# The second stage's last norm moved into the state-space stage, and a new order of weight casts and of the first unit

## The reference, cut to what matters

```python
x = _layernorm(x + _L0_attn_ref(x, ...))   # A
x = _layernorm(x + _L0_ffn_ref(x, ...))    # B
x = _layernorm(x + _L1_attn_ref(x, ...))   # C
x = _layernorm(x + _L1_ffn_ref(x, ...))    # D

# C: proj = x @ in_proj_w.T, split into gate (8192), xBC (8192 + 2*8*128) and dt (128 heads)
# xBC: causal convolution with 4 taps along the sequence, then silu; split into x, B, C
# dt = clip(softplus(dt + dt_bias)); cs = cumsum(dt * A) within chunks of 128 tokens
# scores = (C . B of the same group) * exp(cs_l - cs_s); y = scores @ (x * dt) + state term + D * x
# out = (y * silu(gate), normalised per group of 1024 channels) @ out_proj_w.T
```

## Time and profile before

| | |
|---|---|
| median of 3 runs | 2188.53 us (2187.5 to 2189.29) |
| profiled execution | 2190.99 us |
| its span | 2188.9 us |
| PE busy | 2121.9 us (97%) |
| VectorE busy | 1721.2 us (79%) |
| ScalarE busy | 1239.7 us (57%) |
| GpSimd busy | 688.5 us (31%) |
| mean granted PE clock | 0.987 |

### The profile page before, as it was taken

The page is one execution under the profiler, slowest core; times in us unless marked ns, Lnnn a source line. Parts: engine busy times, 40 slices in busy tenths (PEclk is TensorE's granted clock), DMA queues, the critical chain, the costliest instruction groups (busy, mean ns, idle before and its releaser), DMA issues. The chain is left out here.

```text
span 2188.9 us, 35859 instructions
## 1 busy us (share of the span) xinstructions
PE 2121.9 (97%) x10933; PEld 1691.8 (77%) x10933; DVE 1721.2 (79%) x2943; ACT 1239.7 (57%) x2216; POOL 688.5 (31%) x419
## 2 busy tenths in 40 slices
PE   9999999989999999999999999999999999988997
PEld 7888778868777777777777777777777777766775
DVE  7554446468778888898888888888888888888886
ACT  3222225433377677677767767677777767753232
POOL 5644334311122323324233333324233333330000
PEclk9999999999999999999999999999999999999999
DMA  5312404123231212222132122222221221212433
GB/s 191 113 51 87 159 7 138 58 55 114 98 102 51 91 52 67 73 69 68 49 92 61 55 78 64 68 64 77 61 71 58 68 83 49 74 38 97 144 123 108
DMA packets 126578, 176.40 MB, mean 81 GB/s; under 512 B 17748, under 2 KB 83796, under 8 KB 126068
## 3 DMA queue, kind: packets, MB, share of 16 engines
q1 hardware_dynamic: 126452, 175.07, 25.6%
HBM read 165.72 MB, written 9.31 MB: 80 GB/s over the span
## 5 line engine op out<-in xcount | busy, mean ns | idle before, releaser
L72 PE MATMUL bank<-xT_hi,C_w_hi 128*128 128x512 f32 x1160 | 473.6, 408 | 7.9 <-POOL C_w_lo L1658 7.5
L73 PE MATMUL bank<-xT_lo,C_w_hi 128*128 128x512 f32 x1160 | 459.9, 396 | 0.0
L74 PE MATMUL bank<-xT_hi,C_w_lo 128*128 128x512 f32 x1160 | 459.8, 396 | 0.0
L1658 POOL TENSOR_TENSOR C_w_lo<-C_raw,C_w_hi 128x512 fp32r<-128x512 f32 x130 | 180.5, 1389 | 789.6 <-ACT C_w_hi L1752 746.2
L1365 DVE SCALAR_TENSOR_TENSOR C_acc<-bank,C_par,C_acc 128x510 f32<-128x510 f32 (+2 forms) x384 | 281.2, 744 | 60.4 <-ACT C_acc L1712 37.7
L1481 DVE TENSOR_TENSOR C_decay<-C_decay,C_cb 128x512 f32<-128x512 f32 x384 | 291.9, 789 | 4.8 <-ACT C_decay L1838 4.8
L72 PEld LDWEIGHTS bank<-xT_hi,C_w_hi 128*128 128x128 f32 x1160 | 220.4, 190 | 62.7 <-POOL C_w_lo L1658 8.8
L74 PEld LDWEIGHTS bank<-xT_hi,C_w_lo 128*128 128x128 f32 x1160 | 220.1, 190 | 51.7
L73 PEld LDWEIGHTS bank<-xT_lo,C_w_hi 128*128 128x128 f32 x1160 | 220.9, 190 | 45.3
L72 PE MATMUL bank<-C_out_hi,C_yg_hi 128*128 128x512 f32 x512 | 202.1, 395 | 7.4 <-DVE C_yg_lo L1451 4.0
L74 PE MATMUL bank<-C_out_hi,C_yg_lo 128*128 128x512 f32 x512 | 201.3, 393 | 0.0
(11 more groups left out here) (268 smaller groups left out, 4326.8 us busy)
## 6 DMA issues: line engine op xcount, KB each, us to landing
C_raw<-in_Cxg SPq DMA_DIRECT2D x65, 512.0 KB, 3.6
C_cs_second<-cs_rows SPq DMA_DIRECT2D x64, 512.0 KB, 4.7
C_raw_out<-in_Cout SPq DMA_DIRECT2D x64, 256.0 KB, 2.8
ahead_raw<-in_D SPq DMA_DIRECT2D x32, 512.0 KB, 3.6
front_raw<-in_A SPq DMA_DIRECT2D x20, 512.0 KB, 4.3
B_stat_raw<-in_D SPq DMA_DIRECT2D x16, 512.0 KB, 3.6
ahead_raw<-in_D SPq DMA_DIRECT2D x32, 256.0 KB, 2.6
cb_rows<-C_decay SPq DMA_DIRECT2D x8, 768.0 KB, 3.2
```

Source lines behind the costliest of these rows:

```text
L72: pe.matmul(out, lh, rh, start=start, stop=False)
L73: pe.matmul(out, lh, rl, start=False, stop=False)
L74: return pe.matmul(out, ll, rh, start=False, stop=stop)
L1658: e.tensor_tensor(w_lo[:, slot, :], raw_at, f32(w_hi[:, slot, :]), ALU.subtract).then_inc(lo_done, 1)
```

## The change

Three things. (1) Stage B ends after its last sums, with 8 filler matmuls in place of 12; the norm of its second half is done in stage C with a new `HalfNorm`, `early`. PE makes dt and tile 0 for the first half of the tokens, then the transposes of the norm, waits for all low parts, and makes dt and tile 0 for the second half. (2) VectorE casts the weights of tile i + 2 right behind the convolution of tile i, ahead of the other steps of that place, and tile 2's ahead of the first convolution. The first unit's x weights are cast ahead of tile 15's taps. (3) In unit 0 the correlation products of group 7 are moved between the two halves of the convolution; ScalarE does its second silu after the decays, the second group of exponentials (`second_exp`) after the gate silus, and waits for the store of group 7 only ahead of the exponentials that overwrite its buffer; PE makes the masked products between the two halves of the gate product.

```diff
@@ -737,7 +737,7 @@
             half_sum(1)
-            if kind == "A":
+            if kind != "D":
                 return
 ...
@@ -745,9 +745,6 @@
                 norms[1].scale(v, t)
-            if kind != "D":
-                for k in range(KT):
-                    norms[1].low(v, k, sh.bank[k])
 ...
@@ -955,13 +952,11 @@
                 a2_copy(1)
+            if kind != "D":
                 return
 ...
                 norms[1].scale_shift(a, t)
-            if kind != "D":
-                for k in range(KT):
-                    norms[1].high(a, k, sh.bank[k])
 ...
@@ -1107,9 +1102,7 @@
             if kind == "B":
-                keep_busy(pe, sh, sh.bank[4], 12)
-                for k in range(KT):
-                    norms[1].turn(pe, k, sh.bank[k])
+                keep_busy(pe, sh, sh.bank[4], 8)
     if kind == "B":
 ...
@@ -1174,6 +1167,7 @@
         norm = HalfNorm(sh, ctx, "CN", 0)
+        early = HalfNorm(sh, ctx, "CE", 1)
         bank = sh.bank
 ...
@@ -1247,6 +1241,7 @@
         MS_BANK = 7
+        EARLY_BANK = (6, 7, 2, 3)
 ...
@@ -1523,9 +1518,17 @@
+            for t in range(HT):
+                early.stats_of(v, t, False)
+            early.spread(v)
             v.wait_ge(S.dtw_in, 16)
             v.tensor_copy(w_hi[:, 1, :], raw_out[:, 0, :]).then_inc(S.dtw_hi, 1)
+            early.invert(v)
+            for t in range(HT // 2):
+                early.scale(v, t)
             bc_high(0)
+            for k in range(KT):
+                early.low(v, k, bank[EARLY_BANK[k]])
             v.memset(ones[:, :], 1.0).then_inc(S.ones_set, 1)
 ...
@@ -1545,17 +1548,19 @@
             dt_next = dt_steps()
+            bc_high(1)
             for i in range(2 * GROUPS):
-                if i + 1 < 2 * GROUPS:
-                    bc_high(i + 1)
+                if i == 0:
+                    bc_high(2)
                 bc_conv(i)
+                if 0 < i < 2 * GROUPS - 2:
+                    bc_high(i + 2)
                 if i in (1, 2, 3):
 ...
                     move_cb(i // 2 - 1)
-            move_cb(GROUPS - 1)
             v.wait_ge(S.par_in, 16)
 ...
@@ -1564,6 +1569,8 @@
                 for h in range(2):
+                    if u.first and h == 1:
+                        move_cb(GROUPS - 1)
                     v.wait_ge(S.tap, U * 2 + (h + 1))
 ...
@@ -1725,6 +1732,11 @@
+            early.root(a)
+            for t in range(HT // 2, HT):
+                early.scale_shift(a, t)
+            for k in range(KT):
+                early.high(a, k, bank[EARLY_BANK[k]])
             a.wait_ge(S.consts_in, 32)
 ...
@@ -1761,14 +1773,14 @@
                     chunk_ends()
+                if i == 2 * GROUPS - 1:
+                    a.wait_ge(S.in_bc, 4 * GROUPS - 2)
+                    x_weights(0, 0)
                 bc_tap(i, 0)
 ...
                 bc_silu(i, 0)
-                if i == 2 * GROUPS - 1:
-                    a.wait_ge(S.in_bc, 4 * GROUPS - 2)
-                    x_weights(0, 0)
             bc_silu(2 * GROUPS - 1, 1)
 ...
@@ -1820,14 +1832,14 @@
-
                 for h in range(2):
                     for b in range(BATCH):
+                        if u.first and h == 1 and b == 2:
+                            a.wait_ge(S.cb_stored1, 8 * GROUPS)
                         if h == b == 0:
 ...
                                 a.wait_ge(S.cb_stored0, 8 * GROUPS)
-                                a.wait_ge(S.cb_stored1, 8 * GROUPS)
                             a.wait_ge(cs_in[u.j], (u.U - u.j) * 8 + 16)
 ...
@@ -1837,6 +1849,9 @@
                                  bank[6 + h][:, :].rearrange("p (b l) -> p b l", b=BATCH), ACT.Exp).then_inc(S.decays, 1)
+
+            def second_exp(u):
+
                 for h in range(2):
 ...
@@ -1864,15 +1879,21 @@
                 x_silu(u, 0)
-                x_silu(u, 1)
                 if not u.first:
+                    x_silu(u, 1)
                     y_high(u, 0)
 ...
                 decay_exp(u)
+                if u.first:
+                    x_silu(u, 1)
+                else:
+                    second_exp(u)
                 gate_silu(u, 0)
 ...
                 gate_weights(u.U + 1, 1 - u.j)
+                if u.first:
+                    second_exp(u)
                 if not u.first:
 ...
@@ -1897,10 +1918,10 @@
         def _(pe):
-            def in_bc(i):
+            def in_bc(i, halves=(0, 1)):
                 s = i % 2
                 pe.wait_ge(S.bc_w_lo, i + 1)
-                for h in range(2):
+                for h in halves:
                     wait(pe, S.bc_conv, 6 * (i - 2) + 3 * h + 3)
 ...
@@ -1937,8 +1958,14 @@
                 products(pe, bank[4 + h][:, :], 1, h).then_inc(S.dt_mm, 1)
+                in_bc(0, (h,))
+                if h == 0:
+                    for k in range(KT):
+                        early.turn(pe, k, bank[EARLY_BANK[k]])
+                    pe.wait_ge(early.x_ready, KT)
             for i in range(2 * GROUPS):
-                in_bc(i)
+                if i:
+                    in_bc(i)
                 if i in (5, 7, 9, 11, 13):
 ...
@@ -2068,12 +2095,11 @@
                 in_g(u, 0)
-                if u.group_ended:
+                if u.first:
+                    seg(u, 0)
+                if u.group_ended or u.first:
                     seg(u, 1)
                 in_g(u, 1)
-                if u.first:
-                    seg(u, 0)
-                    seg(u, 1)
                 if not u.first_pair:
 ...
```

## The result

| | before | after |
|---|---|---|
| median of the runs | 2188.30 us (2186.13 to 2190.19, 9 runs) | 2182.66 us (2179.84 to 2185.45, 9 runs) |
| profiled execution, span | 2190.99, 2188.9 | 2183.42, 2181.3 |
| mean granted clock | 0.987 | 0.990 |

The ratio is 0.9974, with 95% between 0.9966 and 0.9982: 5.6 us faster. The forecast was 2178.0, 10.5 us faster. The time lies inside the range for 8 in 10 (2172 to 2183), near its upper end, and outside the forecast's own 2175.5 to 2180.5. In the profiled pair the difference is 7.6 us.

What follows compares the result with a forecast made beforehand. PE was taken as the bound, with gaps and low clock to win: 2.3 us at the start plus 8.2 by the first units, 10.5 off 2188.53, median 2178.0; own range 2175.5 to 2180.5, 8 in 10 2172 to 2183.

Steps and rivals of the forecast that it cites:

- Part 1: Between stages B and C: norm beside C's first loads; with the tile-loop casts 5.4 us at full clock, 2.3 after low-clock charges.
- R: Start of C: the time PE goes on with the second half of dt after the norm's low parts, put at 457.8.
- the gap inside: Start of C: PE's wait for the norm's low parts before the second half of dt, about 2.1 us.
- Part 2: Loop over B and C tiles: earlier casts, VectorE late next; with the moved norm 5.4 us at full clock, 2.3 after charges.
- the wait for GpSimd at tile 4: Loop over B and C tiles: a GpSimd wait at tile 4 or behind would show the prediction wrong; no size given.
- Part 3: Before the first unit: x weights cast ahead of tile 15's taps, 3.30 us of wait plus 2.51 of clock, 5.8 us earlier.
- Part 4: First unit's new order: unit 1's transposes at 614.35, not 623.68; 9.3 us, less 1.1 of low clock, 8.2.
- A switch costs its drain too: ScalarE's two added table switches in the first unit cost 1.4 us each, leaving 7.7 us gained, 2180.8; chance 0.04.
- Nothing is won at the start: Start of C: gaps before R all drop the clock, VectorE's chain begins as late; 8.2 us gained, 2180.3; chance 0.17.
- The clock holds: All new PE gaps: none drops the clock level; 5.4 + 9.3 = 14.7 us gained, median 2173.8; chance 0.17.
- A new wait in the first unit: Store and load of group 7 take twice their 7.4 us; 3.1 us gained, 2185.4; chance 0.06.
- The low level stays: From start of C to second correlation product: clock never rises between new gaps, kernel 19 us slower, 2207; chance 0.04.

Runs made afterwards that it cites:

- part 1 alone: The kernel before with only the second-half norm moved into stage C and 8 fillers, old cast places and first unit; 2190.72 us, ratio 1.0009.
- after again: The changed kernel run once more with no edit; 2182.03 us, ratio to before 0.9968.
- the filler: The changed kernel with the early norm's small tensors allocated last, plus 14 unread matmuls in PE's gap before the second correlation product; 2178.54 us, ratio to before 0.9953.
- the kernel of the casts: The kernel before with only the earlier weight casts, in the B and C tile loop and for the first unit's x weights; 2182.96 us, ratio 0.9971.
- the padded kernels: The kernel before with unused tensors of 176, 16 or 64 bytes a partition; 2191.59, 2189.79 and 2180.99 us, ratios 1.0013, 1.0010 and 0.9962.
- unit 0 alone: The kernel before with only the new order of work in the first unit; 2184.33 us, ratio 0.9980.
- The two opposite edits: The changed kernel with the early norm's small tensors allocated last, ratio to before 0.9964; the kernel before with 176 unused bytes a partition, 1.0013.

## Why the prediction was right in its parts, and where it failed

**Part 1.** C's filler was put at 443.36, its first main matmul at 448.25, R at 457.8, the first convolution at 468.1; they came at 443.05, 447.73, 457.25 and 467.60, after a start that was itself 0.27 earlier. The 2.1 us taken for the gap inside were 1.90. Two charges were wrong: for the gaps ahead of 448.25 and of dt half 1 the sum had 1.2 and 0.8 us of low clock, and this execution shows none (granted 1.00 from 447.5 to 456). It is a charge that comes and goes: part 1 alone paid 1.55 at the first of these places, and after again 1.54 at the second.

**Part 2.** That VectorE is what is late next was right. From the first convolution to the end of the fourth the forecast had 26.5 us; it was 490.50 + 4.52 - 467.60 = 27.4. The term missed is 0.95 us for a scan that shares its time with a low part. The second correlation product came at 495.87, the forecast with its 2.0 us of low clock would say 497.45, without it 495.45. PE was early by 3.40 (forecast 3.5). The clock behind that gap cost 2.73 by after itself (512.91 - 495.87 = 17.04, against 14.31 for the next pair), 2.55 by the filler, 1.7 in after again and 0.2 to 0.3 in the kernel of the casts, where 1.1 was taken: the bounds of 0 and 2.5 were nearly right, and the value for this execution was not. That the lead is 2.1, and 2.3 was the forecast, is luck: two charges that were not paid and one that was more than doubled cancel. In after again the lead there is 1.4.

What the sum did not see is that part 2 alone brings most of this: VectorE's chain starts late in either case, and part 1 moves it by 2.2 us at most (469.84 - 467.60), of which a low level at the start can take nearly all: 0.5 were left in after again, 0.3 in part 1 alone. Nor did it see the wait for GpSimd at tile 4, 0.80 us at 486.58, which the prediction had named as a sign of being wrong. It cost nothing here, since PE waits 3.40 us for VectorE behind it.

**Part 3.** 5.8 us from the wait for tile 15's low part and its clock: 7.9 - 2.1 = 5.8, as forecast. The 2.51 of clock in it is the price in before's execution; behind the same 3.30 us gap the padded kernels and that of unit 0 paid 0 to 2.7.

**Part 4.** The wait for silu 1 was put near 2 us and was 1.70, the one at unit 1 at 1.9 and was 1.79. The lead at unit 1 was forecast as 10.5 and is 10.4. So close a fit is luck in part, for before's 623.68 is the latest of its four executions with the same instructions. No drain: the activation at 597.95 stands 1.30 us behind the start of its table load, with 1.28 of the load itself in between. The 1.4 us per switch of the Trainium skill ("ScalarE: Activation LUTs", What ACT_TABLE_LOAD costs) is not seen: the trace of after speaks against it, as the earlier trace rows did.

**The step that failed** is the last sentence of part 4: "Unit 2 and all behind it have PE as the bound, as before". PE is the bound, but not as before: 62 units take 2.6 us more (1322.00 against 1319.39). An allocation of 176 bytes was costed at nothing because it has no instruction. The two opposite edits, in after and in before, show that it is this, and the starts show in which matmuls. Among the rivals none had it: all were about waits and the clock.

By the profiled pair the account closes: 10.4 at unit 1, less 2.6, is 7.8 at unit 63, and 7.6 in the span. The medians differ by 5.6 only. Before's profiled execution lay 2.7 above its median, after's 0.8; so 1.9 us of the forecast's miss of 4.9 is the scatter of single executions around their medians, and 2.6 the placement. The scatter goes with the clock: of the 23 executions of before timed with after again, those above 2190 us had a mean granted clock of 0.986 to 0.988, those under 2187 one of 0.989 or 0.990.

**The rivals.** The nearest in time are "A switch costs its drain too" (2180.8) and "Nothing is won at the start" (2180.3), both for a wrong reason: the drain is not there, and the start did win 2.1 (1.4 in after again). "The clock holds" is wrong for the 3.40 us gap, right for the two at the start in this execution. "A new wait in the first unit" fell: the store and load of group 7's products decided nothing, PE waited 1.70. "The low level stays" fell: by 512.91 a pair takes 14.31 at a granted clock of 1.00.

## What to carry to other kernels

Read the pace of the longest loop, turn to turn, in both traces before crediting a gain at its head: 0.04 us in a unit is invisible in a timeline and took a quarter of the gain here. A new tensor, however small, moves all that are allocated behind it; put it last, or try the kernel once with an unused pad, for 64 bytes were worth at least as much as the whole change. And when a wait of the bounding engine goes, look for the chain that is late next and take out of it what nobody needs yet: moving the dt steps back brought 3.3 us that neither the norm nor the casts could reach.

## What the runs showed of the hardware

**Placement in SBUF.** The same instructions took 1314.22 us (64 bytes), 1319.39 (none), 1322.31 (176) and 1322.39 (16) for 62 units. In all four the granted clock is 1.00 from 650 to 1900. The loss and the gain lie in the distance between the starts of the matmuls that multiply `xT` by `C_w` (232.1 ns for those of `xT_lo` and `C_w_hi`, 234.1 with 176 bytes, 227.7 with 64); those of `C_out_hi` and `C_yg_lo` move the other way, from 229.4 to 227.7 with 176. What it is that PE loses is not settled. The Trainium skill ("SBUF — State Buffer", SBUF: two separate sides) has PE's ports wait for nobody; no run here tells whether this loss is a wait of another kind.

**The clock behind a gap is no fixed price.** Behind 3.40 and 3.44 us it was low (0.67 and 0.63 in the 8 us from 496, much of it at 1.2 GHz and not 2.4); behind 3.42 in the kernel of the casts it was 1.00, and the first product took 1.99 instead of 3.78 us. Behind a wait of 3.30 us before tile 15 the 24 matmuls took 5.71 us (16 bytes), 7.03 (64 bytes), 7.25 (unit 0 alone), 8.19 (before), 8.34 (176 bytes) and 8.41 (part 1 alone). Behind one of 2.21 us the next 24 took 5.71 us in after and 7.26 in part 1 alone. So it belongs in a range with both ends.

**VectorE beside GpSimd.** The scan took 3.24 us beside a low part and 2.29 without it. The same excess of 0.95 stands in the operation of L1418 (`C_group_out`, two inputs in SBUF): 1.64 us at 495.72 in after, beside a low part from 495.43, and 0.69 in before (L1423 there, at 497.00), with none beside it. An operation on 128x4 (L179 at 446.49) took 1.20 us beside the low part of 1.26 from 446.41; in before, with none beside it, the norm's took 0.16. The Trainium skill ("SBUF — State Buffer", SBUF: two separate sides) says that a VectorE operation with two inputs in SBUF and a GpSimd operation that reads SBUF take a shared pair of ports one after the other; the scan's 0.95 us more, near the 1.09 that a low part takes alone, agree. The scan's case was tested by moving the cast; the other two are read from the traces only.
